# Softmax denominators inverted on ScalarE by logarithm and exponential in two of five attentions

## The reference

```python
s = jnp.einsum('bhqe,bhke->bhqk', q, k) * (1.0 / math.sqrt(D_MODEL))
if causal:
    s = jnp.where(mask, s, -jnp.inf)
w = jax.nn.softmax(s, axis=-1)            # exp(s - max) / sum
o = jnp.einsum('bhqk,bhke->bhqe', w, v)
```

## Time and profile before

| | us |
|---|---|
| median of three runs | 1542.49 |
| lowest, highest | 1541.67, 1547.12 |
| profiled execution | 1547.2 |
| its span | 1545.4 |
| PE busy in it | 1471.7 (95%) |
| DVE busy | 761.3 (49%) |
| ACT busy | 652.2 (42%) |
| mean granted clock of PE | 0.991 |

### The profile page before, as it was taken

The page is one execution under the profiler, slowest core; times in us unless marked ns, Lnnn a source line. Parts: engine busy times, 40 slices in busy tenths (PEclk is TensorE's granted clock), DMA queues, the critical chain, the costliest instruction groups (busy, mean ns, idle before and its releaser), DMA issues.

```text
span 1545.4 us, 28674 instructions
## 1 busy us (share of the span) xinstructions
PE 1471.7 (95%) x12202; PEld 946.0 (61%) x12202; DVE 761.3 (49%) x1591; ACT 652.2 (42%) x1394; POOL 261.4 (17%) x443
## 2 busy tenths in 40 slices
PE   9999899999899999999999999999899999989998
PEld 7665465565555566555677765554566666655576
DVE  1576766767733355111243432325677777752132
ACT  2565555656644433111333432225545444443244
POOL 1443200101000010000122210000245544510000
PEclk9999999999999999999999999999999999999999
DMA  4321000000000100000200000000000000020032
GB/s 163 105 60 40 11 29 2 1 2 2 2 28 1 72 11 1 21 0 0 82 1 1 1 1 28 0 1 7 28 2 2 2 2 2 2 81 0 0 97 62
DMA packets 19562, 36.85 MB, mean 24 GB/s; under 512 B 2058, under 2 KB 17386, under 8 KB 18282
## 3 DMA queue, kind: packets, MB, share of 16 engines
q1 hardware_dynamic: 19434, 35.01, 6.8%
HBM read 33.36 MB, written 1.64 MB: 23 GB/s over the span
## 4 chain that ended last, share of the span: by engine, by line
PE 87%; DVE 6%; ACT 5%; issue 1%; DMA 0%; SPq 0%; DVEq 0%; ACTq 0%
PE psum L447 39%; PE psum L863 11%; PE psum L497 8%; PE psum L593 6%; PE psum L633 6%; ACT probs L1203 3%; PE psum L589 3%; PE psum L532 2%; DVE maxima L1564 2%; PE psum L968 2%; PE psum L996 1%; PE psum L977 1%; PE psum L961 1%; PE psum L1009 1%; PE psum L549 1%
## 5 line engine op out<-in xcount | busy, mean ns | idle before, releaser
L1564 DVE TENSOR_REDUCE maxima<-psum 100x2 f32<-100x722 f32 (+3 forms) x332 | 245.7, 760 | 125.6 <-PE psum L532 98.7
L447 PE MATMUL psum<-x_resid,weights 128*128 128x400 f32 x832 | 294.2, 503 | 3.8 <-ACT probs L1203 2.2
L447 PEld LDWEIGHTS psum<-x_resid,weights 128*128 128x128 f32 x832 | 157.1, 191 | 119.8 <-issue 4.8
L1203 ACT ACTIVATE probs<-psum 128x800 f32<-128x800 f32 (+3 forms) x224 | 168.0, 787 | 101.7 <-PE psum L593 101.6
L863 PE MATMUL psum<-weights 128*128 128x400 f32 x512 | 174.8, 499 | 0.7 <-DVE maxima L1564 0.7
L447 PE MATMUL psum<-weights,ctx_t 128*128 128x256 f32 (+1 forms) x576 | 157.3, 397 | 3.1 <-ACT ctx_t L1125 2.4
L863 PEld LDWEIGHTS psum<-weights 128*128 128x128 f32 x512 | 97.2, 190 | 75.1 <-DVE maxima L1564 0.8
L497 PE MATMUL psum<-ctx_t,weights 128*128 128x361 f32 x384 | 138.4, 486 | 1.6 <-DVE weights L1839 0.8
L447 PEld LDWEIGHTS psum<-weights,ctx_t 128*128 128x128 f32 (+1 forms) x576 | 100.4, 186 | 43.5 <-issue 9.4
L1125 ACT ACTIVATE weights<-psum 128x400 f32<-128x400 f32 (+2 forms) x80 | 37.9, 475 | 205.8 <-PE psum L447 205.7
L633 PE MATMUL psum<-probs,values 128*32 128x100 f32 (+5 forms) x3328 | 111.6, 252 | 2.8 <-ACT q_then_o L1125 1.8
(11 more groups left out here) (167 smaller groups left out, 2073.2 us busy)
## 6 DMA issues: line engine op xcount, KB each, us to landing
weights<-in_w SPq DMA_DIRECT2D x2, 3072.0 KB, 9.6
staged<-in_ctx SPq DMA_DIRECT2D x32, 128.0 KB, 2.1
values<-in_ctx SPq DMA_DIRECT2D x32, 128.0 KB, 2.1
weights<-in_w SPq DMA_DIRECT2D x3, 1024.0 KB, 4.8
weights<-in_src SPq DMA_DIRECT2D x1, 2368.0 KB, 14.5
weights<-in_w SPq DMA_DIRECT2D x1, 2048.0 KB, 7.7
weights<-in_tw SPq DMA_DIRECT2D x2, 1024.0 KB, 5.0
staged<-in_ctx SPq DMA_DIRECT2D x16, 105.0 KB, 2.3
```

What stands on the lines that cost most here:

```text
L447: i = nc.tensor.matmul(PS[0:rows, bk, 0:n], lhs, rhs, start=k == 0, stop=k == len(terms) - 1)
L1203: nc.scalar.activation(PT[0:kn, k % PROBS_KEPT, :, 0:n], PS[0:kn, bk:bk + 2, 0:n], ACT.Exp).then_inc(act_results, mark("act", f"{t} p{b} { ...
L1564: nc.vector.reduce_max(top, src, AX).then_inc(dve_results, mark("dve", f"{t} m{b} {j}"))
```

## The change

In attention 1 (all entries) and attention 2 (all but the last entry) the reciprocal on DVE goes; at `n1` ACT takes the logarithm of `denoms` in place, waits for it, and takes the exponential of minus that. DVE's product at `n1` waits for ACT. Attention 2 has another order string, and its query products begin one slot later. The last entry of attention 2 is normalised behind the stage and keeps the reciprocal.

```diff
-    "c0": "T0 T1 T2 n0 P1 n1 R0 R1 V0 R2 R3 T3 V1 T4 R4 R5 T5 F T6 T7 F K0 V2 K1 F X p0",
+    "c0": "T0 T1 P1 n0 R0 T2 R1 V0 n1 R2 R3 T3 V1 F T4 R4 R5 T5 F T6 V2 T7 K0 F K1 X p0",
...
-PRE_AT = {"s0": 11, "c0": 1, "s1": 4, "c1": 3, "c2": 1}
+PRE_AT = {"s0": 11, "c0": 2, "s1": 4, "c1": 3, "c2": 1}
...
+        def act_dens(act, t, b):
+            if due(f"{t} sw{b}"):
+                act.wait_ge(dve_results, at(f"{t} sw{b}"))
+            nc.scalar.activation(DN[:, :, :], DN[:, :, :], ACT.Ln).then_inc(act_results, mark("act", f"{t} ln{b}"))
+            if due(f"{t} ln{b}"):
+                act.wait_ge(act_results, at(f"{t} ln{b}"))
+            nc.scalar.activation(DN[:, :, :], DN[:, :, :], ACT.Exp, scale=-1.0).then_inc(act_results, mark("act", f"{t} rc{b}"))
...
+                        elif kind == "n" and n == 1 and ATT[t]["narrow"] and (b or t == "c0"):
+                            act_dens(act, *((t, b - 1) if b else ("s0", B - 1)))
...
-                    if due(f"{t} sw{b}"):
-                        dve.wait_ge(dve_results, at(f"{t} sw{b}"))
-                    nc.vector.reciprocal(DN[:, :, :], DN[:, :, :]).then_inc(dve_results, mark("dve", f"{t} rc{b}"))
+                    if (t, b) == ("c0", B - 1):
+                        if due(f"{t} sw{b}"):
+                            dve.wait_ge(dve_results, at(f"{t} sw{b}"))
+                        nc.vector.reciprocal(DN[:, :, :], DN[:, :, :]).then_inc(dve_results, mark("dve", f"{t} rc{b}"))
                 if 1 in parts:
                     if due(f"{t} rc{b}"):
-                        dve.wait_ge(dve_results, at(f"{t} rc{b}"))
+                        dve.wait_ge(producer(f"{t} rc{b}"), at(f"{t} rc{b}"))
```

## The result

| | before | after |
|---|---|---|
| median, us | 1542.49 | 1551.63 |
| lowest, highest, us | 1541.08, 1547.12 | 1550.05, 1556.41 |
| profiled execution, its span, us | 1547.2, 1545.4 | 1550.2, 1548.5 |
| runs | 7 | 7 |

The ratio is 1.0064, with a 95% interval of 1.0048 to 1.0079: the change costs 0.64%, 9 to 10 us. The forecast was 1544.6 us and "no change", with 0.5% as the least that would count; 1551.63 lies inside the range (1534.5 to 1553.5), close to its upper end, and on the side to which I had given 0.12.

The account below looks back on a forecast made before the run. PE, busy 95% of the span, was taken as the bound; attention 1 +4.85, clock +1.0 and attention 2 -3.8 sum to +2.05, giving 1544.6 us on the median, range 1534.5 to 1553.5 for 8 in 10.

Parts of the forecast that it names:

- reciprocals gone from DVE: Both attentions: 31 reciprocals, 43.5 us of DVE, leave; worth 0 to 0.2 us a step, taken as 0.
- the pair on ACT: Logarithm and exponential at 0.43 us each, 0.03 between, 0.89 in all; bounds 0.7 (halved row, 0.35 each) and 1.2.
- attention 1: The product waits for ACT's pair, so PE's scores come late in six steps: +4.85 us, bounds +2 and +8.
- clock: Attention 1, step at 102 us: idle of 2.65 us may bring half clock; 0.6 of 1.7, +1.0, bounds 0 and 3.4.
- attention 2: New order: R0 earlier -0.78, R2 later +0.64, V2 between T6 and T7 -0.47; sum -3.8 us, bounds -10 and +1.
- The upper bound of +8: Attention 1's cost if the two instructions on ACT take 1.2 us.
- the mean and the query's wait: Attention 2, three steps: the wait of 0.60 us behind the query evacuation goes, -0.67 each with its gap.
- R2's wait: Attention 2: R2 waits for both probabilities, 2.67 us behind R0, +0.64; the inverse is free there, room 0.97.
- Rival 1: Order pays, inverse hidden: attention 1 costs 2, attention 2 gives 11; 1533.5 us, chance 0.17.
- Rival 2: Chain over ACT decides, at attention 1's product: +8, clock falls +3.4, attention 2 0; 1554 us, chance 0.12.
- rival 4: Table loads on ACT: 62 at 1.28 us, 79 us in all; 1622 us, chance 0.01.
- rival 3: Nothing moves: reciprocal and pair off the path, the order only shifts waits; 1542.5 us, chance 0.10.

Follow-up runs that it names:

- inverse_only: Against the kernel before: ACT takes the inverse in both attentions, with attention 2's old order; 1570.65 us, ratio 1.0178.
- order_only: Against the kernel before: attention 2's new order and query slot, with the reciprocal on DVE everywhere; 1554.33 us, ratio 1.0067.
- s0_idle_pair: Kernel before plus a logarithm and an exponential of 128x192 on ACT at `n1` in attention 1, on an array nobody reads; 1542.49 us, ratio 1.0000.
- s0_only: Against the kernel before: inverse on ACT in attention 1 alone, with the old order of attention 2; 1551.56 us, ratio 1.0053.
- p0_mid: Kernel before with the last half of attention 2's products with the values moved into the next step, between T1 and T2; 1541.06 us, ratio 0.9983.
- s0_early: Changed kernel with attention 1's pair on ACT right behind V0's evacuation, some 6 us earlier; 1551.91 us, ratio 1.0060 against the kernel before.
- f_back: Attention 2 as changed, but F slots and query products back in place; attention 1 as before except its last entry; 1541.56 us, ratio 0.9983 against before.

## Why the prediction was right and wrong

| term | predicted | measured |
|---|---|---|
| reciprocals gone from DVE | 0 | about 0 in the old order (in inverse_only the late probabilities, 1.29, account for the whole 1.27); 9.3 in the new one (order_only against after) |
| the pair on ACT | 0.89 each | 0.77 |
| attention 1 | +4.85 | +3.7 |
| clock | +1.0 | +1.8, not clear of noise |
| attention 2 | -3.8 | +2.6 |
| sum | +2.05 | +8.1 |

The time lies in the range, but 7 us from the forecast, and the largest part of that is attention 2's (-3.8 predicted, +2.6 measured), the one term of the sum that had the wrong sign.

- **Attention 1 was right in its mechanism**, step by step: 0.73, 0.43, 1.26, 0.43, 1.26 and 0.74 were predicted, and 0.54, 0.23, 1.05, 0.24, 1.05 and 0.50 measured, with 0.08 in one step costed at 0. Each is about 0.2 too high; 0.12 of it is the pair. The wait before L549 grew from 1.42 to 2.48, for 2.7 predicted, and s0_idle_pair shows that it is the late product, as the prediction put it, and not ACT's load. The upper bound of +8 does not follow from its reason: 1.2 for the pair adds 0.31 in each of six steps and gives 6.7.
- **The clock** came out higher than predicted. The idle of 2.48 us at 107.96 is the one to which I had given 0.6 of a fall. In the change's profiled execution there was none, in s0_only's there was one behind the same idle, at the same step (windows of the two kernels, s0_only first):

```profile
108.00:110.00 2.00, 2.00 (x5) 0.90 (x4) 1.16 (x2) 0.00 (x0) 0.46 (x1) 0.50 0.00 0
```

```profile
108.00:110.00 2.00, 2.00 (x23) 1.26 (x24) 0.83 (x1) 0.88 (x3) 2.00 (x4) 1.00 0.02 4
```

  The step was 1.61 us longer for it. The four kernels with attention 1's product behind ACT or the pair moved lost 11.8 to 13.8 us to the clock in the mean, the kernel before 10.0. But p0_mid, which leaves attention 1 alone, lost 12.8, so that the link to these idles is not shown. Nor does the length of the idle before a fall decide it, as the prediction's reading of the trace (behind 1.98 us and more, not under 1.5) suggests. In the kernel before, one of attention 1's falls came at 178.6 us, and the idles of the 10 us ahead of it were of 0.68 us and less:

```profile
178.60:182.00 3.40, 3.40 (x7) 1.85 (x6) 2.61 (x5) 0.32 (x1) 0.00 (x0) 0.50 0.00 0
```

  In s0_early there was a fall at 107.0 us, right behind an idle of 1.43 us, the one that had no such end in the kernel before (1.42).
- **Attention 2 is the step that failed**, in sign. By kinds of steps, with a query product that changed its step taken out at 1.34 us (of the steps with output products, that with two query products takes 18.77 us before, and that with none 16.09):

| steps | predicted | measured |
|---|---|---|
| 4 with output products, the opening with the first | 0 | +2.6 |
| 3 with the mean and the query's wait | -2.0 | -1.0 |
| 4 with further norm products | 0 | +0.7 |
| 3 plain | -1.8 | -1.0 |
| the last but one of the stage | 0 | +1.2 |

  In a plain step the parts are: T0 to R0 1.46 (1.50 predicted, 2.28 before), R0 to R2 2.78 (2.67 predicted, 2.03 before), and V2 between T6 and T7 -0.26 instead of -0.47; the step takes 14.41 us, for 14.13 predicted and 14.74 before. The direction of each is as predicted, the first gain by 0.04 larger, the price by 0.11 larger, and V2's gain by 0.21 smaller. The last is a term that the prediction left out: V2 takes 1.05 us between T6 and T7, and had taken 0.86 between K0 and K1. In the output steps I had counted -0.22 for V2, where no wait stood that it could cover: the output products already covered T6 and T7. Measured there is +0.46 for V2 and the parting of T6 from T7 (f_back), and T5's wait for DVE came in, 0.41 (0.55 predicted). With both, each output step is 0.65 us longer, where I had 0.19. Of the steps with one norm product, as the prediction calls them, the first group's second step has four products (L447 x4 at 225.66 us in the kernel before) where its like have two; before, they covered the waits of both T6 and T7. Ahead of T4 they cover nothing, which makes that step +0.69 where the others have +0.02. The last but one step I had counted with its like, and overlooked that there V2 had covered X's wait for the last maxima.
- **The reciprocal's price** was read in the old order only. There DVE has room for it. In the new order the same instruction costs 9.3 us (11.9 less 2.6), so the change's second half needs its first; and its first needs the second still more (19.3 less 2.6). The prediction treated the inverse as free inside R2's wait, and that holds in the new order, where ACT still stood idle 0.30 us between the pair and the next probabilities.
- **Rivals.** Rival 1 (the order pays) fell: f_back shows that this order with F where it was is worth 0. Rival 2 is right in its mechanism and its place, with 3.7 for 8; the outcome, slower by 0.6%, is nearer to its 1554 than to my 1544.6, but through attention 2, which it had at 0. No table load, so rival 4 fell, and rival 3 with the result. I gave slower too little: gains from covered waits were taken in full, and the measured +2.6 of attention 2 lies outside its own bounds (-10 to +1). That the total still fell into the range is owed to the width of the range and to attention 1's smaller loss, not to attention 2's account.

What stays open: what brings the falls of the clock, and whether the kernels with the inverse on ACT in attention 1 really lose more to them. Why V2 takes 0.19 us more between T6 and T7 was not pursued.

## What to carry to other kernels

An instruction moved to a less busy engine costs what stands behind it in that engine's order and what waits for it: the same pair of 0.77 us cost 0 beside the chain, 3.7 us over seven steps in it, and 1.27 in every step where it also made its engine wait for another, with the probabilities queued behind. Price both edits of a coupled change in each other's order, and count a gain from filling a wait only where a wait stands in that very kind of step, less what the moved work costs in its new place. The cheap win here was found in the rows of before: two short waits that recur in most steps, each filled with work that was already there, for 11 us of the stage and 9.4 us of the mean time.

## What the runs showed of the hardware

- Step times of kernels with the same local order agree to 0.01 or 0.02 us between programs; all that varied beside were the steps with falls of the clock. A fall of 3.4 us lengthened its step by 1.6 to 1.7 us where PE was busy throughout.
- The same idle of 2.47 or 2.48 us was followed by 1.2 GHz in one program and by 2.4 GHz in another. The Trainium skill (TensorE: Matmul & The Clock Gate, A second HAM failure mode) warns of short idles between groups of products; the added idles here did not bring a fall each time, and over all runs their programs lost 1.8 to 3.8 us more to the clock than the kernel before, as did p0_mid (3.1), which adds none in attention 1.
- Two score tokens of two products each (L532, 32x361) took 0.29 us together, and 0.28 us each with V2 between them (f_back and the kernel before, near 256 us).
- Logarithm and exponential of 128x200, SBUF to SBUF, took 0.37 us each with 0.03 between, and of 128x192 in bfloat16 0.36. The halved row of the prediction (0.35) was nearer than the value that I took.
